# Causal mask of the pair attention: added by VectorE while it reads the scores, in place of four tensor products per step

## Chip, cores and metric

The kernel runs on 1 core of one Trainium2 chip. The metric is the device time of one execution in microseconds (us); several runs of a kernel are summed up by their median. The engines are TensorE (PE: matmuls, with its weight loads shown apart as PEld), VectorE (DVE), ScalarE (ACT), GpSimd (POOL) and SyncE (SP, which starts DMAs here). They run side by side and wait for each other on semaphores. Each engine works through its own instructions in program order.

## The reference

A tower of four transformer layers over 32 images of 37 tokens (36 patches and a class token), width 256, float32. Only two of its eight blocks after the embedding matter here: the attentions of layer 0 and of layer 2, both causal with 16 heads of 16 columns.

```python
# layer 0 (layer 2 is the same up to names and the layout of its weights)
att = jnp.einsum('bhqd,bhkd->bhqk', q, k) * (1.0 / jnp.sqrt(jnp.float32(D)))
causal = jnp.tril(jnp.ones((T, T), bool))
att = jnp.where(causal, att, -jnp.inf)
att = jax.nn.softmax(att, axis=-1)
y = jnp.einsum('bhqk,bhkd->bhqd', att, v)
...
h = _layernorm(h + _L0_attn_ref(h, ...), axis=-1)
```

## The kernel before

`tower` runs nine stages one after the other, separated by barriers: 0 the embedding, then attention and feed-forward block of each layer. `pair_attention` is stage 1 (layer 0, from about 36 to 142 us) and stage 5 (layer 2, from about 483 to 593 us).

**How the work is tiled.** An image has T = 37 rows; R = 111 rows are three images. `pair_attention` takes the 32 images in 16 pairs, one pair per step `s`; in the partition dimension one image of the pair stands in rows 0 to 36 and the other in rows 64 to 100 (PR = 101). Six images, three steps, are a unit `u = s // 3`. There are 18 steps (STEPS): a pair's work is spread over three steps, and the steps of different pairs overlap. All 16 heads of a pair have their scores at once, in four banks of PSUM (`scores`: 4 banks x 4 heads x 37 keys, 592 columns per row).

**What one pair needs, in order.** PE writes the scores (`score`: four matmuls that put the mask, 0 or -1e30, into the four banks, then 16 small matmuls that add the products of queries and keys). DVE takes each row's maximum (L469) and writes scores minus maximum to `P` in SBUF (L472); this is `shift`. ACT takes the exponential in place (`exps`, L412). PE transposes `P` in two halves (`p_T`, L613), ACT copies each half out (L417), PE multiplies with the values (`values`, L626), DVE divides by the sums (`normalise`, L480 and L483), PE transposes the result (`o_T`, L635), ACT copies it (L423).

**What a unit needs beside it.** PE: the transpose of the next unit's input (`x_T`, L555, step 3k), its query products (`q_project`, L563, step 3k), its key products (L563, step 3k+1) and its value products in two phases (`v_project`, L586, step 3k+2), and the output product of the unit before (`o_project`, L646, step 3k+1). DVE: `v_out` (L495, four additions, step 3k+2), which brings the values to SBUF, and `residual` (L504 to L510, step 3k+1 after the shift): residual and layer norm statistics. POOL: `norm` and `biased` (L358 to L363, L352), the layer norm of the unit before and its copy with a bias. Steps 3k, 3k+1 and 3k+2 are called x step, o step and v step below.

**What sets the order.** It is written out by hand, per engine. On PE a step is: `score(s)`, `p_T(s-1, 0)`, the unit's work, `o_T(s-2)`, `p_T(s-1, 1)`, more of the unit's work, `values(s-1)`. On DVE: `normalise(s-2)`, `shift(s)`, the unit's work. On ACT: copy of `p_T(s-1, 0)`, then others, copy of `o_T(s-2)`, copy of `p_T(s-1, 1)`, `exps(s)`. `score(s)` may overwrite the four banks once `shift(s-1)` has read them (semaphore `shifted`, which also releases the exponential).

Two things are in stage 1 alone: DVE prepares weights of the next stage (maxima L1679 in steps 3 and 4, 2.25 us each; conversions L541, with ACT's L455, in steps 12 to 16). In stage 5 alone PE transposes rows for a router (`routed_T`, L658) in step 16, which waits until all 16 shifts are done.

The mask comes by DMA with the stage's weights as `pair_mask` (101 x 37, float32). At the stage's start DVE converts it to bfloat16, four times side by side (L463), as the operand of the four matmuls.

## Time and profile before

| | |
|---|---|
| median of 3 runs | 1130.23 us (1118.12, 1130.23, 1132.64) |
| profiled execution, its own time | 1124.02 us |
| its span in the trace | 1122.2 us |
| mean granted TensorE clock | 0.898 |
| busy: PE / DVE / ACT / POOL | 963.6 / 590.2 / 487.1 / 321.8 us |
| mask matmuls L596 | 128, 14.7 us busy (a mean of 237 ns while they overlap) |
| score matmuls L603 | 16.0 us busy |
| shift: L469 and L472 | 24.6 us and 24.8 us busy, 32 of each |
| exponential L412 | 23.1 us busy, 32 |

The profile is one execution. A timeline row merges instructions of one kind that follow each other: start, the time from its first start to its last end, engine, line, what is written and read, and the count (a float32 matmul stands in it as two). Neighbouring rows of PE overlap by a little since matmuls are pipelined, so the distance from one start to the next is the time that a group costs. `[idle before <-releaser]` tells that the engine stood still and who ended it.

### The profile page before, as it was taken

Reading aid. Unit: us, or ns where it says so; the run is one execution under the profiler, and the core shown is the slowest. Engines: PE = TensorE matmul, PEld = TensorE weight load, DVE = VectorE, ACT = ScalarE, POOL = GpSimd, SP = SyncE. Lnnn points to the kernel's source line nnn. Section 1 sums busy time; section 2 is a strip of 40 time slices with the busy share of each in tenths; the row PEclk is TensorE's granted clock in tenths of the full one; section 3 lists DMA queues with packets and bytes.
Section 4 is the critical chain, followed back from the end, with each engine's and each line's share of the span. In section 5 each row is a group of like instructions: output and inputs, shape, how many; then the busy total and the mean of one; then the engine's idle time right before and its main releaser. Section 6 shows DMA issues by size and latency. Waiting matters only on the chain. (4 is left out here: it accounts for less than half of the span.)

```text
span 1122.2 us, 25634 instructions
## 1 busy us (share of the span) xinstructions
PE 963.6 (86%) x10184; PEld 719.9 (64%) x10184; DVE 590.2 (53%) x1279; ACT 487.1 (43%) x907; POOL 321.8 (29%) x423
## 2 busy tenths in 40 slices
PE   6899867899999799879996899999579999988664
PEld 6788625677777566658873466665267777777332
DVE  5576667566665298735656122211355456432585
ACT  3444477555555497634440122222113334422454
POOL 0213302444431000031320344442444545431101
PEclk9999888898999898889996899999788999986885
DMA  6200030200000100040007352332400000000001
GB/s 215 82 3 2 3 118 1 80 2 1 0 0 2 45 0 1 1 155 3 3 2 279 142 150 46 48 48 24 124 9 3 2 2 4 3 3 1 1 1 44
DMA packets 19657, 46.29 MB, mean 41 GB/s; under 512 B 4546, under 2 KB 10882, under 8 KB 18686
## 3 DMA queue, kind: packets, MB, share of 16 engines
q1 hardware_dynamic: 14300, 37.36, 9.4%
q0 software_dynamic: 4992, 6.82, 3.9%
q8 instruction: 79, 1.29, 0.5%
q10 hardware_dynamic: 256, 0.57, 0.2%
q14 instruction: 30, 0.25, 0.1%
HBM read 37.62 MB, written 7.12 MB: 40 GB/s over the span
## 5 line engine op out<-in xcount | busy, mean ns | idle before, releaser
L2620 DVE TENSOR_TENSOR weights_even<-psum,weights_even 128x512 f32<-128x512 f32 x26 | 18.0, 692 | 104.9 <-PE psum L2692 104.9
L2415 POOL DMA_INDIRECT expert_sums<-weights_even,L2f_target x26 | 41.1, 1583 | 93.2 <-DVE weights_even L2613 80.8
L1046 PE MATMUL psum<-L_cT,weights_odd 128*128 128x222 f32 (+1 forms) x192 | 49.5, 392 | 9.6 <-DVE L_by_sin L935 8.4
L2291 PE MATMUL psum<-weights_even,L1f_H 128*111 128x256 f32 x176 | 46.8, 424 | 7.5 <-DVE L1f_H L2222 7.5
L935 DVE TENSOR_TENSOR L_by_cos<-psum,vectors_odd 128x444 f32<-128x444 f32 (+1 forms) x48 | 26.6, 554 | 49.4 <-PE psum L1046 49.0
L2449 ACT ACTIVATE weights_even<-psum 128x256 f32<-128x256 f32 x26 | 10.0, 383 | 96.3 <-PE psum L2687 93.2
L2692 PE MATMUL psum<-gate_weights,weights_even 128*128 x104 | 50.8, 612 | 0.5 <-ACT weights_even L2449 0.5
L2725 PEld LDWEIGHTS psum<-L2f_EW,weights_even 128*128 128x128 f32 x208 | 39.4, 190 | 17.0 <-issue 13.0
L2725 PE MATMUL psum<-L2f_EW,weights_even 128*128 x208 | 49.2, 379 | 0.8 <-ACT weights_even L2454 0.8
L2692 PE MATMUL psum<-L2f_EW,weights_even 128*128 x104 | 49.9, 603 | 0.0
L874 ACT ACTIVATE L_PT<-psum 101x296 f32<-101x296 f32 x32 | 13.3, 416 | 80.7 <-PE psum L1087 80.0
L417 ACT ACTIVATE L_PT<-psum 101x296 f32<-101x296 f32 x64 | 26.9, 421 | 48.9 <-PE psum L613 48.9
L2291 PEld LDWEIGHTS psum<-weights_even,L1f_H 128*111 128x111 f32 x176 | 34.8, 200 | 18.4 <-DVE L1f_H L2222 8.7
L1046 PEld LDWEIGHTS psum<-L_cT,weights_odd 128*128 128x128 f32 x192 | 36.0, 215 | 15.8 <-issue 13.4
L358 POOL TENSOR_TENSOR L_rs<-L_mv,ln_eps 111x2 f32<-111x2 f32 (+1 forms) x12 | 3.0, 252 | 143.4 <-DVE L_mv L510 136.3
L155 PE MATMUL psum<-identb 128*128 128x512 bf16 x162 | 43.9, 434 | 0.0
L563 PE MATMUL psum<-L_xT,weights_odd 128*128 128x222 f32 (+1 forms) x192 | 41.0, 361 | 3.3 <-DVE L_V L495 1.9
L165 PE MATMUL psum<-decay_W_high,L1a_xT_high 128*111 128x512 f32 x88 | 39.3, 447 | 0.9 <-DVE L1a_xT_low L1344 0.9
L1119 PE MATMUL psum<-weights_odd,L_OT 128*111 128x256 f32 x176 | 39.2, 380 | 0.5 <-ACT L_OT L881 0.5
L613 PE MATMUL psum<-ident,L_P 101*101 101x101 f32 x256 | 37.1, 268 | 1.9 <-ACT L_PT L417 1.2
L800 POOL TENSOR_TENSOR L_P<-L_P,L_rc 101x592 f32<-101x592 f32 x16 | 19.2, 1198 | 68.2 <-DVE L_rc L953 68.2
L2273 PE MATMUL psum<-L1f_XT,weights_even 128*128 128x333 f32 (+1 forms) x128 | 36.9, 434 | 1.3 <-ACT L1f_XT L2114 0.7
(449 smaller groups left out, 2586.9 us busy)
## 6 DMA issues: line engine op xcount, KB each, us to landing
L2f_EW<-experts SPq DMA_DIRECT2D x16, 512.0 KB, 8.0
weights_even<-L_w SPq DMA_DIRECT2D x4, 1024.0 KB
gate_weights<-experts SPq DMA_DIRECT2D x8, 512.0 KB, 6.9
patch_ring<-patches SPq DMA_DIRECT2D x11, 333.0 KB, 7.0
weights_odd<-L_wqkv SPq DMA_DIRECT2D x2, 768.0 KB
out<-X SPq DMA_DIRECT2D x10, 111.0 KB
expert_rows<-X SPq DMA_DIRECT2D x1, 1056.0 KB, 4.9
expert_sums<-X SPq DMA_DIRECT2D x1, 1056.0 KB
```

Source lines behind the costliest of these rows:

```text
L155: core.nc.tensor.matmul(cols(core.bank(bank), 4, 128), core.identb[:], core.identb[:].unsqueeze(1).broadcast_to([128, 4, 128]), start=True ...
L165: mm = core.nc.tensor.matmul(out, left[a], right[b], start=first and n == 0, stop=last and n == len(passes) - 1)
L417: nc.scalar.activation(PT[:PR, s % 2, 4 * half:4 * half + 4].rearrange("p n (b q) -> p n b q", b=2), cols(core.bank(PTB)[:PR, 0:512], 4, 1 ...
L563: mm = nc.tensor.matmul(bank[:, c * NC2:c * NC2 + n], wqkv[:, kd, first + 128 * c:first + 128 * (c + 1)], xT[:, u % 2, kd, 0:n], start=kd ...
L613: mm = nc.tensor.transpose(core.bank(PTB)[:PR, 128 * i:128 * i + PR], P[:PR, s % 2, 2 * cq:2 * cq + 2].rearrange("p e k -> p (e k)")[:, 0: ...
L1046: mm = nc.tensor.matmul(bank[:, h * NC2:h * NC2 + width(u)], wu[:, (2 * g + h) * 128:(2 * g + h + 1) * 128], cT[:, u % 2, n // 4, 0:width( ...
L1119: mm = nc.tensor.matmul(core.bank(M2)[:R, m * D:(m + 1) * D], OT[:, c, first:first + R], wo[:, c, :], start=c == 0, stop=c == 7)
L2273: mm = nc.tensor.matmul(core.bank(bank)[:, 0:k * R], w1[:, kk, c * 128:(c + 1) * 128], XT[:, kk, group_cols(t0, k)], start=kk == 0, stop=k ...
L2291: mm = nc.tensor.matmul(y_bank(t), H[:, c, t * R:(t + 1) * R], w2[:, c, :], start=False, stop=c == nf - 1 and (t % 2 == 1 or t == NT - 1))
L2415: nc.gpsimd.indirect_dma_start(sums[:, :], bass.IndirectOffsetOnAxis(ap=target[:, j:j + 1], axis=0), Y[:, j % 2, :], None, compute_op=ALU. ...
L2692: mm = nc.tensor.matmul(core.bank(bank), xsT[:, j % 2, c, :], weights[:, expert[j], c * NF:(c + 1) * NF], start=c == 0, stop=c == KD - 1)
L2725: mm = nc.tensor.matmul(core.bank(5)[:, 0:D], HT[:, (j - 1) % 2, c * 128:(c + 1) * 128], EW[:, expert[j - 1], KD * NF + c * D:KD * NF + (c ...
```

## The change

Four edits in `pair_attention`, so in stages 1 and 5 alike:

- `score` loses its four mask matmuls; the 16 score matmuls start their own sums (`start=True, stop=True`).
- `shift` has three DVE instructions instead of two: scores plus mask, PSUM and SBUF to `P` (new L471); the row maximum of `P` (L473); `P` minus the maximum, in place (L475). A drain stands behind the first and the second.
- A semaphore `masked`, raised by the first of them, releases `score(s+1)`; it was `shifted`, raised by the last. The wait for `pt_ps` moves from ahead of the last instruction to ahead of the first.
- At the stage's start the conversion of the mask goes; DVE clears the four banks instead, once.

```diff
-        mask = sb("mask", [128, 4, T], BF16)
+        mask = w["pair_mask"]
...
-                nc.vector.tensor_copy(mask[:PR], w["pair_mask"].unsqueeze(1).broadcast_to([PR, 4, T])).then_inc(set_up, 1)
+                nc.vector.memset(scores, 0.0).then_inc(set_up, 1)
...
                     peaks = mx[:PR, s % 2].rearrange("p (j h) -> p j h", j=4)
-                    nc.vector.tensor_reduce(peaks, scores, AX.X, ALU.max)
+                    whole = P[:PR, s % 2].rearrange("p (j h) k -> p j h k", j=4)[:, :, :, 0:T]
+                    after(dve, pt_ps, 2 * (s - 1))
+                    nc.vector.tensor_tensor(whole, scores, mask.unsqueeze(1).unsqueeze(1).broadcast_to([PR, 4, 4, T]), ALU.add).then_inc(masked, 1)
                     dve.drain()
-                    after(dve, pt_ps, 2 * (s - 1))
-                    nc.vector.tensor_tensor(P[:PR, s % 2].rearrange("p (j h) k -> p j h k", j=4)[:, :, :, 0:T], scores,
-                                            peaks.unsqueeze(3).broadcast_to([PR, 4, 4, T]), ALU.subtract).then_inc(shifted, 1)
+                    nc.vector.tensor_reduce(peaks, whole, AX.X, ALU.max)
+                    dve.drain()
+                    nc.vector.tensor_tensor(whole, whole, peaks.unsqueeze(3).broadcast_to([PR, 4, 4, T]), ALU.subtract).then_inc(shifted, 1)
...
-                    after(pe, shifted, s)
-                    for j in range(4):
-                        nc.tensor.matmul(core.bank(S0 + j)[:PR, 0:4 * T], core.identb[:PR, :PR], mask[:PR].rearrange("p h k -> p (h k)"),
-                                         start=True, stop=False)
+                    after(pe, masked, s)
...
-                                                      start=False, stop=c == 1)
+                                                      start=True, stop=True)
```

PE of the kernel before, from the end of an o step through a v step to `o_T` of the next x step (here steps 4 to 6; L586 are the value products, L635 is `o_T`):

```order
L626 MATMUL psum<-L_V,L_PT 37x34 x16
L596 MATMUL psum<-L_mask,identb 101x148 x4
L603 MATMUL psum<-L_kT,L_qT 37x74 x16
L613 MATMUL psum<-ident,L_P 101x101 x4
L586 MATMUL psum<-weights_odd,L_xT 37x128 x12
L635 MATMUL psum<-ident,L_O 128x101 x2
L613 MATMUL psum<-ident,L_P 101x101 x4
L586 MATMUL psum<-weights_odd,L_xT 37x128 x12
L626 MATMUL psum<-L_V,L_PT 37x34 x16
L596 MATMUL psum<-L_mask,identb 101x148 x4
L603 MATMUL psum<-L_kT,L_qT 37x74 x16
```

The same stretch in the changed kernel:

```order
L625 MATMUL psum<-L_V,L_PT 37x34 x16
L602 MATMUL psum<-L_kT,L_qT 37x74 x16
L612 MATMUL psum<-ident,L_P 101x101 x4
L588 MATMUL psum<-weights_odd,L_xT 37x128 x12
L634 MATMUL psum<-ident,L_O 128x101 x2
L612 MATMUL psum<-ident,L_P 101x101 x4
L588 MATMUL psum<-weights_odd,L_xT 37x128 x12
L625 MATMUL psum<-L_V,L_PT 37x34 x16
L602 MATMUL psum<-L_kT,L_qT 37x74 x16
```

Each step has four matmuls less; nothing else of PE moved.

DVE of the kernel before, from `residual` of an o step through the v step to the next `normalise`, whose result `o_T` waits for (here steps 7 to 9, the first unit without the maxima of the weights; L495 is `v_out`):

```order
L504 TENSOR_TENSOR L_z<-psum,L_xb 111x512
L507 BN_STATS L_stat<-L_z 111x6 x2
L510 BN_AGGR L_mv<-L_stat 111x2 x2
L480 RECIPROCAL L_rd<-psum 101x16
L483 TENSOR_TENSOR L_O<-psum,L_rd 101x256
L469 TENSOR_REDUCE L_mx<-psum 101x16
L472 TENSOR_TENSOR L_P<-psum,L_mx 101x16x37
L495 TENSOR_TENSOR L_V<-psum,vectors_odd 37x24x16 x4
L480 RECIPROCAL L_rd<-psum 101x16
L483 TENSOR_TENSOR L_O<-psum,L_rd 101x256
```

And in the changed kernel:

```order
L506 TENSOR_TENSOR L_z<-psum,L_xb 111x512
L509 BN_STATS L_stat<-L_z 111x6 x2
L512 BN_AGGR L_mv<-L_stat 111x2 x2
L482 RECIPROCAL L_rd<-psum 101x16
L485 TENSOR_TENSOR L_O<-psum,L_rd 101x256
L471 TENSOR_TENSOR L_P<-psum,vectors_odd 101x16x37
L473 TENSOR_REDUCE L_mx<-L_P 101x16
L475 TENSOR_TENSOR L_P<-L_P,L_mx 101x16x37
L497 TENSOR_TENSOR L_V<-psum,vectors_odd 37x24x16 x4
L482 RECIPROCAL L_rd<-psum 101x16
L485 TENSOR_TENSOR L_O<-psum,L_rd 101x256
```

`shift` has one instruction more, of 592 columns like the other two, and its last one now reads two operands in SBUF (`P` and the maxima) where it read one in PSUM and one in SBUF.

## Rows read from the trace of the kernel before

**Rows 1.** The page's head: span and number of instructions.

```profile
span 1122.2 us, 25634 instructions
```

**Rows 2.** Stretches: from:to, length, busy us (instructions) by engine, PEclk, DMA, GB/s.

```profile
70.00:80.00 10.00, 8.68 (x207) 7.52 (x202) 9.45 (x18) 3.56 (x11) 4.77 (x6) 1.00 0.01 3
500.00:510.00 10.00, 8.55 (x131) 7.30 (x131) 4.49 (x8) 4.69 (x12) 0.00 (x0) 0.83 0.01 2
```

**Rows 3.** Timeline of PE, one unit of stage 5: start us, us, work [idle before].

```profile
522.12 0.46 PE L596 MATMUL psum<-L_mask,identb 101*101 101x148 bf16 x4
522.51 0.49 PE L603 MATMUL psum<-L_kT,L_qT 32*37 32x74 f32 x32
...
529.23 0.34 PE L635 MATMUL psum<-ident,L_O 101*128 101x101 f32 x2
529.61 0.57 PE L613 MATMUL psum<-ident,L_P 101*101 101x101 f32 x4
...
533.23 0.60 PE L613 MATMUL psum<-ident,L_P 101*101 101x101 f32 x4
...
538.59 0.46 PE L596 MATMUL psum<-L_mask,identb 101*101 101x148 bf16 x4
```

**Rows 4.** Timeline of DVE, the same unit.

```profile
521.53 0.69 DVE L504 TENSOR_TENSOR L_z<-psum,L_xb 111x512 f32<-111x512 f32 x1 [2.96 <-PE psum L646]
...
523.95 0.77 DVE L469 TENSOR_REDUCE L_mx<-psum 101x16 f32<-101x592 f32 x1
...
525.48 1.11 DVE L495 TENSOR_TENSOR L_V<-psum,vectors_odd 37x384 f32<-37x384 f32 x2
527.14 1.12 DVE L495 TENSOR_TENSOR L_V<-psum,vectors_odd 37x384 f32<-37x384 f32 x2 [0.55 <-PE psum L586]
...
528.63 0.43 DVE L483 TENSOR_TENSOR L_O<-psum,L_rd 101x256 f32<-101x256 f32 x1
```

**Rows 5.** Groups by line: out<-in, shapes, xcount | busy us, mean ns | idle before.

```profile
L472 DVE TENSOR_TENSOR L_P<-psum,L_mx 101x592 f32<-101x592 f32 x32 | 24.8, 776 | 2.8 <-issue 0.4
L469 DVE TENSOR_REDUCE L_mx<-psum 101x16 f32<-101x592 f32 x32 | 24.6, 770 | 7.4 <-PE psum L603 6.3
...
L951 DVE TENSOR_REDUCE L_rc<-L_P 101x16 f32<-101x592 f32 x16 | 12.3, 770 | 46.4 <-ACT L_P L869 46.4
...
L1386 DVE TENSOR_TENSOR L1a_la_low<-L1a_la,L1a_la_high 111x512 fp32r<-111x512 f32 x11 | 7.6, 693 | 5.5 <-ACT L1a_la_high L1317 5.5
...
L412 ACT ACTIVATE L_P<-L_P 101x592 f32<-101x592 f32 x32 | 23.1, 721 | 1.5 <-DVE L_P L472 1.5
```

**Rows 6.** Timeline of POOL, the same unit.

```profile
524.70 2.43 POOL L363 TENSOR_SCALAR X<-L_z,L_mv,L_rs 111x256 f32<-111x256 f32 x2 [0.18 <-issue]
```

**Rows 7.** DVE and POOL side by side: timelines near 198 and 37; L1256's min/median/max.

```profile
198.70 1.21 DVE L1348 TENSOR_TENSOR L1a_W_low<-weights_odd,decay_W_high 128x1024 fp32r<-128x1024 f32 x1
...
198.73 1.98 POOL L1256 TENSOR_SCALAR decay_xin<-decay_xin,L1a_prs 111x256 f32<-111x256 f32 x1 [0.18 <-issue]
...
L1256 POOL TENSOR_SCALAR decay_xin<-decay_xin,L1a_prs x10: 929/966/1982, 198.7 to 329.7; 111x256 f32<-111x256 f32 x10
...
36.72 3.48 DVE L463 CAST L_mask<-vectors_odd 101x148 bf16<-101x148 f32 x1
...
37.28 2.82 POOL L341 MEMSET L_V<- 128x3264 f32 x1
```

**Rows 8.** Timeline of PE at five other places of the two stages.

```profile
46.88 1.74 PE L563 MATMUL psum<-L_xT,weights_odd 128*128 128x222 f32 x8 [0.95 <-DVE L_V L495]
...
74.61 0.39 PE L635 MATMUL psum<-ident,L_O 101*128 101x101 f32 x2 [1.30 <-DVE L_O L483]
...
112.18 0.39 PE L635 MATMUL psum<-ident,L_O 101*128 101x101 f32 x2 [0.35 <-DVE L_O L483]
...
128.57 0.67 PE L613 MATMUL psum<-ident,L_P 101*101 101x101 f32 x4 [0.47 <-ACT L_P L412]
...
577.71 1.74 PE L658 MATMUL psum<-ident,X 111*128 111x111 f32 x16
```

More of the change, by code:

```diff
@@ L308, in pair_attention @@
         stat, mv, rs = sb("stat", [128, 2, 2, 6]), sb("mv", [128, 2, 2, 2]), sb("rs", [128, 2, 2])
-        mask = sb("mask", [128, 4, T], BF16)
+        mask = w["pair_mask"]
         bkm = sb("bkm", [128, 2, 2])
-        (xT_ps, xT_done, q_ps, q_done, k_ps, k_done, v_ps, v_done, s_ps, shifted, exp_done, pt_ps, pt_done, o_ps, o_done,
+        (xT_ps, xT_done, q_ps, q_done, k_ps, k_done, v_ps, v_done, s_ps, masked, shifted, exp_done, pt_ps, pt_done, o_ps, o_done,
          oT_ps, oT_done, y_ps, z_done, var_ready, norm_done, xb_done, zeroed, set_up) = st.sems(
-            "xT_ps xT_done q_ps q_done k_ps k_done v_ps v_done s_ps shifted exp_done pt_ps pt_done o_ps o_done "
+            "xT_ps xT_done q_ps q_done k_ps k_done v_ps v_done s_ps masked shifted exp_done pt_ps pt_done o_ps o_done "
             "oT_ps oT_done y_ps z_done var_ready norm_done xb_done zeroed set_up")
```

## The prediction

> **What bounds the kernel now.** Only two of nine stages change, so I read those two and let the rest of the span stand [rows 1]. The timeline of PE comes first. In the middle of stage 5 a unit of three steps lasts from 522.12 to 538.59, 16.47 us [rows 3], and no row of PE in it has an idle mark: PE bounds there. A mask group costs 522.51 - 522.12 = 0.39 us. Second, DVE of the same unit [rows 4]: it waits 2.96 us before `residual` (521.53), then works almost without a break until `normalise` ends at 528.63 + 0.43 = 529.06; the one pause is 0.55 us before the second half of `v_out`. `o_T` needs that result and starts at 529.23. So the slack of this path is 0.17 us, though DVE idles 3.5 us in these two pauses alone. That is the place which decides. Third, the spots where PE already waits for DVE or ACT [rows 8].
>
> **What is removed.** 32 mask groups (16 steps, two stages) of 0.39 us: 12.5 us if PE bounds everywhere. The conversion at the start of stage 1 took 3.48 us [rows 7], but it was over at 40.20, while PE was still at the first unit's projections (it reaches the second unit's at 46.88 [rows 8]); removing it gives nothing, and clearing the banks, one pass over 592 columns and below 1 us, hides there too.
>
> **What is added on DVE.** The add reads 592 columns from PSUM, as L472 does: 0.776 us. The maximum moves to SBUF: L951 has that very shape in SBUF and takes 770 ns, L469 from PSUM also 770. The last subtraction has two operands in SBUF: L1386 does this on 512 columns in 693 ns; 80 more columns at about 1.04 ns give 776 [rows 5]. Against 1.53 us for a shift (523.95 to 525.48 [rows 4]) that is one instruction of 0.776 and one drain more, which I take as 0.08: **+0.85 us per shift**. Bounds: 0.77 without the drain, 0.93 with two.
>
> The Trainium skill (VectorE: DVE Perf Modes, § The TRN2 errata) gives a Vector instruction a fixed part of 120 cycles when it reads PSUM and 58 when it reads SBUF. By it two of the three would be 0.065 us shorter, and the whole forecast some 1 us lower. The two rows of 770 ns speak against it, and the measurement decides.
>
> **The steady unit.** In the v step the chain `residual`, `normalise`, `shift`, four `v_out`, `normalise` grows by 0.85 and loses the pause of 0.55: +0.30, so the result comes at 529.36 and `o_T` at 529.46 instead of 529.23. PE, with two masks less in front, would be there at 528.45, and waits 1.0 us. Behind `o_T`, `p_T` started at 529.61 since it waited for ACT's copy; now the copy is early and it starts 0.23 after `o_T`, at 529.69: +0.08. So two of three masks are lost to this wait; only the third, at the end of the x step, is kept: -0.39 + 0.08 = **-0.31 us per unit**, where PE alone would give -1.18. The other DVE results have cover. In the x step the shift starts 0.34 after L483's successor, at 529.3, and ends at 529.3 + 2 x 0.85 + 0.78 = 531.78; the exponential takes 0.72 [rows 5], so `p_T` can start at 532.6; PE comes at 533.23 - 0.31 = 532.9. `masked` is raised long before the next score. The o step's shift lies in front of DVE's idle 2.96 us.
>
> **The port.** The new subtraction takes two operands from SBUF, and that has a price when POOL reads too. At 198.73 POOL's L1256 took 1.98 us instead of its usual 0.97, beside DVE's L1348 with two SBUF operands from 198.70 to 199.91: POOL stood until DVE was done [rows 7]. In the steady unit the subtraction comes at 523.95 + 2 x 0.85 = 525.65, inside POOL's first L363 (two of 1.22 from 524.70 [rows 6]), which ends at 525.92. If DVE gets in there, it has lost d = 0.27 us; if it loses to the second too, d = 1.5. Both are to be had by the rows: the conversion at 36.72 lasted until POOL's second memset was over, 40.10, so it lost to one that came later [rows 7]; at 198.70 the waiting engine went as soon as the other ended. I take 0.27, with 0 and 1.5 as the ends. This d adds straight to the chain before `o_T`. It is the rule of the Trainium skill (SBUF — State Buffer, § Who interferes with whom) that a Vector instruction with two SBUF inputs contends with a GpSimd one that reads SBUF, and that each fully blocks; the row at 198.73 agrees.
>
> **Stage 1, added up** (shift of PE against before). The second `v_out` stands behind the first shift, and PE waits for it at 46.88 already [rows 8]: +0.85 less the first mask, with a small gap, +0.54. The masks of steps 1 to 4 give back 1.56, of which a short wait before `o_T` keeps 0.13: -0.89 at the first `residual`. In steps 5 to 7 the maximum of a weight lies in DVE's chain, and PE already waits 1.30 us at 74.61 [rows 8]: the chain keeps its length plus 0.85, so the -0.89 is gone and one mask is left: -0.39. Next unit -0.31 + d: -0.70 + d. In the unit of step 11 PE waits at 112.18 already [rows 8], so nothing is hidden: +0.30 + d at `o_T`, and 0.15 more since the next exponential is late as well: -0.25 + 2d. In steps 14 and 15 two shifts follow each other in DVE's unbroken work, and `p_T` at 128.57 waits for the exponential [rows 8]: +1.70 + d. End of stage 1: **+1.45 + 3d**.
>
> **Stage 5.** The same start without the maxima: -0.94. Two units: -0.62 + 2d. Unit of step 11: the slack is nil, +0.06 + d. Then `routed_T`, at 577.71 [rows 8], waits for the sixteenth shift, two shifts of +0.85 later less 0.17 of slack: it moves from 577.71 to 578.4, +0.70 + d. End: **-0.80 + 4d**.
>
> Together +0.65 + 7d; with d = 0.27: **+2.5 us**. On the profiled execution (1124.02) that gives 1126.5. The four executions shown of before (1118.12, 1124.02, 1130.23, 1132.64) have a mean of 1126.3 and lie 14.5 us apart, more than any case below but one; I add to the mean: 1126.3 + 2.5 = **1129 us**. Measured against the median of 1130.23 it is no change.
>
> **Rivals.**
> - *DVE hides it, PE bounds throughout.* Then all 32 x 0.39 = 12.5 us come back: 1114. For it: DVE's idle 3.5 us per unit. Against it: nearly all of it lies before `residual`, not in front of `o_T`, where the slack is 0.17, and PE waits at 74.61 and 112.18 already. Chance 0.14.
> - *DVE loses the port each time* (slower). With d = 1.5: +0.65 + 10.5 = +11, 1137; if it loses also to L352 behind, d is about 2.9 and the sum +21, 1147. The seven are the v steps 8, 11 and 14 of stage 1 and 5, 8, 11 and 14 of stage 5. It takes d over 3.1 in all of them to pass 2%. For it: the conversion at 36.72; POOL's two L363 follow each other without a gap. Against it: 198.70. Chance 0.16.
> - *TensorE's clock falls in the new waits.* In the stretch from 500 it was granted 0.83 after waits of PE at the start of stage 5; from 70 to 80 it stayed at 1.00 in spite of the wait of 1.30 us [rows 2, 8]. A stretch of 10 us at 0.83 costs 1.7 us; in each of seven units 12 us: 1138. Chance 0.10.
> - *The sum above*, d from 0 to about 0.7 and shift from 0.77 to 0.93: the terms move by 4 us, the scatter of before by 7 to either side. Chance 0.60, own range 1119 to 1138.
>
> **How the numbers follow.** The range of 8 in 10 takes the forecast's scatter, part of the first rival from below and of the two slower ones from above: 1117 to 1143. What a measurement of this kernel can tell from no change is about 2%, 22.5 us. Faster by that needs nearly twice all masks: 0.03, for scatter. Slower needs the port lost throughout, or both slow rivals: 0.05. Within 2%: 0.92.
>
> **What the changed profile would show.** L471, L473 and L475 at 0.77 to 0.78 us each; L475 in v steps longer or late beside L363, and L363 longer. PE idle about 1 us before `o_T` in x steps, put down to DVE's L485; a unit of 16.1 to 16.5 us. If a unit is 15.3 us, the first rival holds; at 17.6 the second. `routed_T` with a wait for L475 in front. Stage 1 ends 1.5 to 3 us later, stage 5 within 1 us. I am wrong at the root if L475 is cheaper than 0.7 us or if DVE's order lets `o_T` through earlier.

## The result and the profile after

The changed kernel was compared with the one before three times, each time with a set of executions of the kernel before taken for that comparison.

| comparison | changed kernel, median us (lowest to highest) | before, median us | ratio, 95% interval |
|---|---|---|---|
| first (4 executions each) | 1141.51 (1135.02 to 1148.13) | 1128.84 | 1.0126 [1.0077, 1.0175] |
| second (12 and 35) | 1135.23 (1130.57 to 1154.78) | 1128.95 | 1.0035 [0.9994, 1.0076] |
| third (12 and 35) | 1133.64 (1130.04 to 1151.81) | 1129.40 | 1.0039 [1.0000, 1.0079] |

So the change costs 4 us (0.35 and 0.39%) by the two larger comparisons, whose intervals just reach 1, and 14 us (1.3%) by the first, which has four executions on each side. The forecast was 1129 us: 2.5 us of added time on a base of 1126.3, called no change against the median of 1130.23. Of every kernel here, the one before too, a part of the executions is 1.5 to 3% longer at a lower granted clock; the comparisons leave these out, which four executions hardly allow, and by their clock the profiled ones of the first comparison (1148.13 us, 0.874) and of the third (0.871), of the changed kernel with fill in all waits (0.883) and of the kernel before with late statistics (0.878) are of that kind, while that of the second (0.887) is not.

The head of the page after ([rows 1] has 25634 instructions and a span of 1122.2 us):

```profile
span 1146.3 us, 25470 instructions
```

VectorE's three instructions of a shift, from the groups by line (shapes, count, busy us, mean ns, idle before):

```profile
L475 DVE TENSOR_TENSOR L_P<-L_P,L_mx 101x592 f32<-101x592 f32 x32 | 25.5, 796 | 2.4
L473 DVE TENSOR_REDUCE L_mx<-L_P 101x16 f32<-101x592 f32 x32 | 24.6, 770 | 2.9
L471 DVE TENSOR_TENSOR L_P<-psum,vectors_odd 101x592 f32<-101x592 f32 x32 | 24.6, 768 | 6.5 <-PE psum L602 6.4
```

All three cost what the prediction had taken. The 796 ns of L475 is a mean with one outlier; 770 to 780 ns is what nearly all of them show. TensorE in the steady unit of stage 5 that answers to [rows 3] (start us, length us, then the work, in brackets the idle time before it and what ended it):

```profile
541.76 0.77 PE L625 MATMUL psum<-L_V,L_PT 101*37 101x34 f32 x32
...
548.40 0.55 PE L557 MATMUL psum<-ident,X 111*128 111x111 f32 x4
549.79 0.39 PE L634 MATMUL psum<-ident,L_O 101*128 101x101 f32 x2 [0.85 <-DVE L_O L485]
...
557.78 0.77 PE L625 MATMUL psum<-L_V,L_PT 101*37 101x34 f32 x32
```

`values` to `values` is 557.78 - 541.76 = 16.02 us, before 16.47. The mask groups are gone, and in front of `o_T` there is the wait of 0.85 us put down to `normalise` (L485), where [rows 3] shows none. VectorE and GpSimd (POOL) in the v step of that unit, answering to [rows 4] and [rows 6]:

```profile
544.28 0.77 DVE L471 TENSOR_TENSOR L_P<-psum,vectors_odd 101x592 f32<-101x592 f32 x1
...
545.98 0.78 DVE L475 TENSOR_TENSOR L_P<-L_P,L_mx 101x592 f32<-101x592 f32 x1
546.68 2.27 DVE L497 TENSOR_TENSOR L_V<-psum,vectors_odd 37x384 f32<-37x384 f32 x4
...
549.31 0.42 DVE L485 TENSOR_TENSOR L_O<-psum,L_rd 101x256 f32<-101x256 f32 x1
```

```profile
545.04 2.81 POOL L363 TENSOR_SCALAR X<-L_z,L_mv,L_rs 111x256 f32<-111x256 f32 x2 [0.18 <-issue]
```

L475 takes 0.78 us beside POOL's L363, and L363's pair takes 2.81 us where [rows 6] has 2.43: POOL stood, not VectorE. Taken one by one, the pair's first instruction, begun at 545.04 before L475, took its usual 1.22 us, and the second, begun at 546.26 while L475 was running, took 1.59.

**Where the time went.** The two changed stages can be measured from their first VectorE instruction (L461) to their last `residual` (L504 before, L506 after). Before:

```profile
36.57 0.23 DVE L461 TENSOR_TENSOR L_bkm<-vectors_odd 128x2 f32<-128x2 f32 x2 [0.69 <-PEq L131]
...
139.79 0.42 DVE L504 TENSOR_TENSOR L_z<-psum,L_xb 111x256 f32<-111x256 f32 x1
...
483.82 0.23 DVE L461 TENSOR_TENSOR L_bkm<-vectors_odd 128x2 f32<-128x2 f32 x2 [0.77 <-PEq L131]
...
589.72 0.42 DVE L504 TENSOR_TENSOR L_z<-psum,L_xb 111x256 f32<-111x256 f32 x1 [4.48 <-PE psum L646]
```

That is 103.22 us in stage 1 and 105.90 us in stage 5. The same in the second comparison's profile of the changed kernel:

```profile
36.53 0.23 DVE L461 TENSOR_TENSOR L_bkm<-vectors_odd 128x2 f32<-128x2 f32 x2 [0.69 <-PEq L131]
...
144.34 0.42 DVE L506 TENSOR_TENSOR L_z<-psum,L_xb 111x256 f32<-111x256 f32 x1 [0.99 <-PE psum L645]
...
492.18 0.23 DVE L461 TENSOR_TENSOR L_bkm<-vectors_odd 128x2 f32<-128x2 f32 x2 [0.77 <-PEq L131]
...
601.25 0.42 DVE L506 TENSOR_TENSOR L_z<-psum,L_xb 111x256 f32<-111x256 f32 x1 [4.34 <-PE psum L645]
```

107.81 and 109.07 us: 4.6 and 3.2 us more. By the same reading:

| profile | stage 1, us | stage 5, us | of it: units from `residual` to `residual` in stage 5 |
|---|---|---|---|
| before | 103.22 | 105.90 | 16.47, 16.47, 15.06, **13.21**, 6.98 |
| changed, first | 113.40 | 109.02 | 16.02, 16.02, 15.17, **17.83**, 6.99 |
| changed, second | 107.81 | 109.07 | 16.02, 16.02, 15.17, **17.84**, 7.01 |
| changed, third | 113.39 | 109.08 | 16.02, 16.02, 15.18, **17.83**, 7.03 |

Three profiles agree within 0.1 us in stage 5: the steady units are 0.45 us shorter each, and the unit from step 13 to step 16 is 4.6 us longer. That unit is where stage 5 loses. The stages 2 to 4, which are the same code, took from 344 us (before, 139.79 to 483.82) over 348 (second profile) to 355 us (first profile, 149.78 to 504.88); no reading below uses them.

Not all of stage 1's 4.6 us is the change's. The first 16 projections of TensorE (L563 before, L565 after) stand ahead of every scores product. In the kernel before, in the second profile of the changed one, and in another kernel that is unchanged up to there (experiment 5), they read:

```profile
37.83 3.27 PE L563 MATMUL psum<-L_xT,weights_odd 128*128 128x222 f32 x16 [0.70 <-ACT L_xT L386]
```

```profile
37.80 4.96 PE L565 MATMUL psum<-L_xT,weights_odd 128*128 128x222 f32 x16 [0.70 <-ACT L_xT L386]
```

```profile
37.73 4.87 PE L566 MATMUL psum<-L_xT,weights_odd 128*128 128x222 f32 x16 [0.69 <-ACT L_xT L386]
```

The same work takes 1.6 to 1.7 us longer at half clock for a part of it: from 36 to 46 us the granted clock is 1.00 in the first, 0.83 in the two others. It came with unchanged code too, so the change need not be its cause, and why it comes in one execution and not in another is open. The same holds for the stage's last unit: 5.35 us before, 6.28 changed, but also 6.29 in the kernel before with late statistics and with one longer wait (experiments 6 and 5), where its last output product takes 2.05 us for 1.32, as in the changed kernel.

TensorE of the first profile in stage 5's unit of 17.83 us:

```profile
593.37 0.49 PE L602 MATMUL psum<-L_kT,L_qT 32*37 32x74 f32 x32
594.77 0.60 PE L612 MATMUL psum<-ident,L_P 101*101 101x101 f32 x4 [0.91 <-ACT L_P L412]
...
596.62 1.07 PE L625 MATMUL psum<-L_V,L_PT 101*37 101x34 f32 x32
597.98 3.22 PE L657 MATMUL psum<-ident,X 111*128 111x111 f32 x16 [0.29 <-DVE L_P L475]
600.99 0.89 PE L612 MATMUL psum<-ident,L_P 101*101 101x101 f32 x4
```

and the stretches around it (from:to, length, busy us with instructions of PE, PEld, DVE, ACT, POOL, then the granted clock), of after and of before:

```profile
585.00:595.00 10.00, 8.71 (x182) 7.16 (x183) 7.66 (x16) 5.12 (x16) 3.67 (x4) 1.00 0.01 2
595.00:605.00 10.00, 9.15 (x73) 7.75 (x73) 3.27 (x7) 4.11 (x12) 0.75 (x2) 0.61 0.01 2
```

```profile
574.00:584.00 10.00, 9.05 (x166) 7.61 (x160) 4.41 (x10) 4.78 (x14) 1.81 (x2) 1.00 0.01 2
```

After the wait of 0.91 us in front of `p_T` (step 15; ACT's exponential is late since VectorE's shift of step 14 is) the clock goes from 1.00 to 0.61 in the mean of ten microseconds, that is to its lower level (1.2 of 2.4 GHz) for most of them. `routed_T` (L657) takes 3.22 us where [rows 8] has 1.74 for the same sixteen transposes, and `p_T` behind it 0.89 where it takes 0.52 at full clock. Before, the stretch that holds `routed_T` was granted 1.00 throughout.

### The profile page after: what moved, and what is told of

It is laid out like the page before. It is cut to its first block and busy times, and to the rows that moved or that the text cites. A ratio compares the mean times of both kernels' runs of the same rounds, so it can differ in the third digit from the quotient of the medians.

```text
span 1146.3 us, 25470 instructions
## 1 busy us (share of the span) xinstructions
PE 977.5 (85%) x10056; PEld 731.8 (64%) x10056; DVE 610.8 (53%) x1311; ACT 489.3 (43%) x907; POOL 324.3 (28%) x423
## 5 line engine op out<-in xcount | busy, mean ns | idle before, releaser
L565 PE MATMUL psum<-L_xT,weights_odd 128*128 128x222 f32 (+1 forms) x192 | 46.7, 399 | 5.3 <-DVE L_V L497 3.9
L565 PEld LDWEIGHTS psum<-L_xT,weights_odd 128*128 128x128 f32 x192 | 39.8, 231 | 7.3 <-issue 4.2
L155 PE MATMUL psum<-identb 128*128 128x512 bf16 x162 | 43.1, 428 | 0.0
L165 PE MATMUL psum<-decay_W_high,L1a_xT_high 128*111 128x512 f32 x88 | 41.9, 476 | 0.9 <-DVE L1a_xT_low L1343 0.9
```

Source lines behind the costliest of these rows:

```text
L155: core.nc.tensor.matmul(cols(core.bank(bank), 4, 128), core.identb[:], core.identb[:].unsqueeze(1).broadcast_to([128, 4, 128]), start=True ...
L165: mm = core.nc.tensor.matmul(out, left[a], right[b], start=first and n == 0, stop=last and n == len(passes) - 1)
L565: mm = nc.tensor.matmul(bank[:, c * NC2:c * NC2 + n], wqkv[:, kd, first + 128 * c:first + 128 * (c + 1)], xT[:, u % 2, kd, 0:n], start=kd ...
```

## The experiments

Three theories. **One**: TensorE's longer waits behind VectorE's longer chain let its clock fall, and that is most of the loss. **Two**: the chain itself costs it, and the falls of the clock are scatter. **Three**: it is the work that TensorE no longer has that brings the clock down. The table that the sections refer to, each from one profile, ratio from the timed executions:

| kernel | stage 1 | stage 5 | steady unit | step 13 to 16 unit of stage 5 | ratio, 95% interval |
|---|---|---|---|---|---|
| before | 103.22 | 105.90 | 16.47 | 13.21 | 1 |
| changed (second) | 107.81 | 109.07 | 16.02 | 17.84 | 1.0035 [0.9994, 1.0076] |
| vector half alone | 108.92 | 106.61 | 16.46 | 13.93 | 1.0037 [0.9996, 1.0079] |
| tensor half alone | 99.72 | 98.65 | 15.29 | 12.55 | 0.9900 [0.9827, 0.9972] |
| changed, fill in all waits | 104.05 | 105.82 | 16.05 | 14.59 | 0.9950 [0.9904, 0.9995] |
| changed, one fill | 107.73 | 104.73 | 16.02 | 13.94 | 1.0019 [0.9983, 1.0055] |
| changed, late statistics | 102.17 | 107.51 | 15.29 | 17.73 | 0.9999 [0.9963, 1.0035] |
| the same, one fill | 102.83 | 103.63 | 15.29 | 13.93 | 0.9979 [0.9945, 1.0014] |
| the same, fill at start and end | 101.37 | 102.07 | 15.29 | 14.71 | 0.9907 [0.9866, 0.9947] |
| before, late statistics | 104.24 | 105.86 | 16.47 | 13.21 | 0.9992 [0.9948, 1.0037] |
| before, fill at start and end | 106.31 | 107.29 | 16.47 | 14.66 | 1.0009 [0.9970, 1.0049] |
| before, one longer wait | 107.17 | 109.49 | 16.46 | 16.89 | 1.0025 [0.9995, 1.0056] |

Stage 1's times differ between kernels by 1.5 to 1.7 us, and once by 3.0, because of its first projections alone. They take 3.27 or 3.28 us in the profiles of before, both halves, fill in all waits, late statistics and late statistics with one fill; 4.80 to 4.96 us in the three of the changed kernel and those with one fill, before with late statistics, before with one longer wait, late statistics with fill at start and end; and 6.29 us in before with fill at start and end. In the profile of before the first `residual` comes 33.29 us after the stage's start, in before with one longer wait 34.89 us, and nothing else of TensorE differs up to there.

**1. The vector half alone.** The changed kernel, with TensorE's four products put back on top:

```
+        maskb = sb("maskb", [128, 4, T], BF16)
...
                     after(pe, masked, s)
+                    for j in range(4):
+                        nc.tensor.matmul(core.bank(S0 + j)[:PR, 0:4 * T], core.identb[:PR, :PR],
+                                         maskb[:PR].rearrange("p h k -> p (h k)"), start=True, stop=False)
```

> The vector half of the change alone: VectorE runs the three instructions (add mask, maximum, subtraction) and releases the scores' banks after the first, but TensorE still multiplies the mask in with its four products (so the mask is added twice, which leaves the result as it was). Theory 1 (TensorE's longer waits behind VectorE's longer chain let its clock fall, and that is most of the loss): as slow as the changed kernel or slower, 1.010 to 1.020 of the kernel before, half clock after longer waits in steps 5 to 12 of stage 1 and at the start of both attention stages. Theory 2 (the chain itself costs everything, 0.85 us per step where it binds, the falls of the clock are scatter): 1.008 to 1.015, with stage 1 longer by the chain at full clock. Theory 3 (less work on TensorE alone brings the clock down): TensorE has all its work here, so no more falls of the clock than before and 1.000 to 1.004.

Measured: 1.0037, below what theories one and two asked for and inside the range of three; it is also as slow as the whole change (1.0035 and 1.0039). The steady unit says why. It is 16.46 us, as before: the mask groups on TensorE cover the 0.85 us that VectorE needs longer, and the waits of `o_T` add up to 7.9 us where the changed kernel has 12.0 and 12.7 in its first two profiles, and the kernel before 4.6. So this kernel does not have "the same waits with more work", as its expectation assumed. In the unit of step 13 to 16 of stage 5:

```profile
584.43 0.60 PE L616 MATMUL psum<-ident,L_P 101*101 101x101 f32 x4
...
587.63 1.74 PE L661 MATMUL psum<-ident,X 111*128 111x111 f32 x16 [0.45 <-DVE L_P L476]
```

The `p_T` of step 15 (584.43) has no wait of note, and `routed_T` takes 1.74 us, full clock. This run does not decide between one and three.

**2. The tensor half alone.** The kernel before without the four products; VectorE has its two instructions. The causal mask is left out here.

```
-                    for j in range(4):
-                        nc.tensor.matmul(core.bank(S0 + j)[:PR, 0:4 * T], core.identb[:PR, :PR],
-                                         mask[:PR].rearrange("p h k -> p (h k)"), start=True, stop=False)
...
-                                                      start=False, stop=c == 1)
+                                                      start=True, stop=True)
```

> The tensor half of the change alone: the four products with the mask are gone and VectorE keeps its two instructions; the causal mask is left out of the computation. Theory 1: TensorE's waits for VectorE grow by at most 0.31 us per step and seldom pass 1 us, so no more falls of the clock than before, and a time of 0.985 to 0.998 of the kernel before. Theory 2: the same, 0.990 to 0.998. Theory 3 (less work on TensorE brings its clock down): stage 1 longer by 5 to 10 us at a clock below 0.9 in its later half, 1.004 to 1.010.

Measured: 0.9900, and the two stages 3.5 and 7.3 us shorter. The steady unit is 15.29 us: 16.47 less three mask groups (1.18). Theory three is out in this form: with the same work taken from TensorE the clock of that unit stays up, and `routed_T` takes its 1.74 us:

```profile
572.30 0.39 PE L632 MATMUL psum<-ident,L_O 101*128 101x101 f32 x2 [0.20 <-DVE L_O L483]
...
574.18 1.74 PE L655 MATMUL psum<-ident,X 111*128 111x111 f32 x16
```

Together the halves say how the parts combine. Over both stages the tensor half gives -10.8 us and the vector half +6.4; their sum would be -4.4, the whole change is +7.8. Of the 12 us between, 3.9 are the half clock behind step 14 (experiment 4) and 1.7 that of the first projections, which neither half's profile has. The rest is what each half covers for the other: TensorE's gain is only there if VectorE's chain does not grow, and the chain's growth is only hidden if TensorE keeps the masks.

**3. Fill in TensorE's waits.** The changed kernel with products that nobody reads (128 x 512, four take 1.04 us) where it waits: six before the second `q_project`, four before `o_T` in steps 6, 9, 12, nine in steps 15 and 16.

```
+                    if s in (15, 16):
+                        pe.wait_ge(z_done, 4)
+                        keep_busy(core, M2, 4 if s == 15 else 3)
                     if 1 <= s <= NP:
                         p_T(s - 1, 0)
...
+                    if s == 15:
+                        keep_busy(core, M2, 2)
+                    if s % 3 == 0 and 3 < s < 15:
+                        pe.wait_ge(v_done, v_phases(u + 1))
+                        keep_busy(core, M2, 4)
                     if s >= 2:
                         o_T(s - 2)
...
+                    if s == 0:
+                        pe.wait_ge(xT_done, 2)
+                        keep_busy(core, M1, 6)
                     if u + 1 < NU and s % 3 == 0:
                         q_project(u + 1)
```

> The changed kernel with products that nobody reads put into TensorE's waits: six before the second projection of Q, four before the transpose of O in the steps 6, 9 and 12, a few in the last steps of both attention stages. VectorE's chain stays as long as in the changed kernel. Theory 1: the clock stays at 0.95 or more from 50 to 130 us, stage 1 takes 108 to 111 us in place of 118, and the time is 0.997 to 1.005 of the kernel before. Theory 2: no gain, 1.011 to 1.018, since the chain is as long and the fill delays the transposes by up to 0.2 us. Theory 3 gives the same as theory 1, but without a fall before the longest waits.

Measured: 0.9950 [0.9904, 0.9995], faster than the kernel before and outside all the ranges named, on the fast side. VectorE's chain is as long as in the changed kernel, and the steady unit stays at 16.05:

```profile
562.87 1.04 PE L155 MATMUL psum<-identb 128*128 128x512 bf16 x4
563.74 0.34 PE L634 MATMUL psum<-ident,L_O 101*128 101x101 f32 x2
```

so what came back is not the chain's length. The unit of step 13 to 16 of stage 5 is 3.2 us shorter in spite of nine products on top, the same unit of stage 1 is 1.75 us shorter (14.82 for 16.57 in the second profile), and stage 1 takes 104.05 us in place of 107.81 to 113.40; 1.5 to 1.7 us of that lie in the first projections, ahead of any fill. This goes against theory two as the whole explanation. It does not explain the time, though: the two stages add up to 209.87 us here and to 209.12 before, so the 5.6 us (0.5%) by which this kernel was timed faster than before are not found in them.

**4. One fill.** Only the four products in front of `p_T` in step 15.

```
+                    if s == 15:
+                        pe.wait_ge(z_done, 4)
+                        keep_busy(core, M2, 4)
                     if 1 <= s <= NP:
                         p_T(s - 1, 0)
```

> The changed kernel with four products that nobody reads in one place of each attention stage: TensorE's wait of 0.91 us before the transpose of P in step 15. Theory 1: that one wait starts the half clock in the last unit of stage 5; with the fill the clock stays at 1.00 there and the last unit takes 13.2 to 14.2 us in place of 17.83, 3 to 4 us less in all than the changed kernel. If other, shorter waits are enough, the last unit stays at 17 us or more.

```profile
581.31 1.04 PE L155 MATMUL psum<-identb 128*128 128x512 bf16 x4
582.28 0.60 PE L612 MATMUL psum<-ident,L_P 101*101 101x101 f32 x4
...
584.14 0.90 PE L625 MATMUL psum<-L_V,L_PT 101*37 101x34 f32 x32
585.49 1.74 PE L657 MATMUL psum<-ident,X 111*128 111x111 f32 x16 [0.45 <-DVE L_P L475]
```

The rows are those of the changed kernel's unit with L155 where the wait of 0.91 us was, and every length is back at full clock: `values` 0.90 for 1.07, `routed_T` 1.74 for 3.22. The unit takes 13.94 us for 17.83, stage 5 takes 104.73 us for 109.07. From 584 to 594 the granted clock is 1.00. The time, 1.0019, is 0.2% below the changed kernel's 1.0035 and 1.0039; the intervals overlap, so for this one the profile carries the verdict. Experiment 7 has the same fill once more, on top of late statistics, with the same effect (17.73 to 13.93). In stage 1 the same fill changed nothing (107.73).

**5. One longer wait in the kernel before.** VectorE's maximum of step 14 is taken three times; nothing else.

```
+                    for _ in range(2 if s == 14 else 0):
+                        nc.vector.tensor_reduce(peaks, scores, AX.X, ALU.max)
+                        dve.drain()
```

> The kernel before with VectorE's maximum of step 14 taken three times in place of once (the result is the same), so that TensorE waits about 1.2 us longer before one transpose of P in each attention stage, while it does all its work, the mask too. Theory 1 (a wait of this length at this place is enough for the half clock): the last unit of stage 5 takes 16.5 to 18.5 us in place of 13.2 and the time is 1.002 to 1.007 of the kernel before. If it takes the missing work as well (theory 3), the clock stays at 1.00, the last unit takes 14.0 to 14.8 us, and the time is at most 1.003.

```profile
577.72 0.77 PE L629 MATMUL psum<-L_V,L_PT 101*37 101x34 f32 x32 [0.29 <-ACT L_OT L423]
579.62 0.43 PE L599 MATMUL psum<-L_mask,identb 101*101 101x148 bf16 x4 [1.14 <-DVE L_P L475]
579.99 0.53 PE L606 MATMUL psum<-L_kT,L_qT 32*37 32x74 f32 x32
580.45 1.00 PE L616 MATMUL psum<-ident,L_P 101*101 101x101 f32 x4
...
584.18 3.16 PE L661 MATMUL psum<-ident,X 111*128 111x111 f32 x16
587.18 0.52 PE L616 MATMUL psum<-ident,L_P 101*101 101x101 f32 x4
```

The wait came out before the mask group of step 15 (1.14 us, [1.14 <-DVE L_P L475]) and not before `p_T`. Behind it `p_T` takes 1.00 us for 0.60 and `routed_T` 3.16 for 1.74; from 587.18 on the lengths are normal again. The unit takes 16.89 us (13.21 before), the kernel 1.0025, which lies in the ranges of both theories, so the unit decides. TensorE does all of its work here, masks too: a wait of that length at that place is enough, and theory three falls. Together with experiment 4 this shows theory one for stage 5: put the wait in and the half clock comes, fill the wait and it goes.

**6. Late statistics.** The other way to take the waits away: an earlier `normalise`. Of `residual` only the addition stays in the o step; the two BatchNorm statistics and aggregations move into the x step two steps later, behind its shift (those of the last units of a stage stay where they were). In stage 1 the maximum of a weight in step 4 also moves ahead of the addition, so the first `residual` stands behind it there.

```
+                def statistics(u):
+                    p, n = u % 2, len(UNITS[u][1])
                     dve.drain()
...
                     if s % 3 == 1 and u >= 1:
                         residual(u - 1)
+                        if s >= 13:
+                            statistics(u - 1)
+                    if s % 3 == 0 and 6 <= s <= 12:
+                        statistics(u - 2)
```

> The changed kernel with VectorE's statistics of the residual (two bn_stats, two bn_aggr) moved from the o step, where they stand ahead of the next steps' work, into the x step that has less to do; the addition itself stays. The wait of the transpose of O in x steps is taken away by an earlier start of VectorE's chain, not by fill. Theory 1: waits of 0.85 to 1.7 us in the middle of the stages go, so do the falls of the clock behind them; unit of stage 5 at 15.2 to 15.9 us (16.02 in the changed kernel), time 0.988 to 1.002 of the kernel before. Theory 2 (the chain alone): the unit gets shorter all the same, 4 to 8 us less than the changed kernel, 1.004 to 1.009. If the addition of 0.85 us has its price in the other steps too, the unit stays at 16.0 and the time at 1.010 or more.

```profile
541.87 0.39 PE L642 MATMUL psum<-ident,L_O 101*128 101x101 f32 x2
...
549.87 0.77 PE L633 MATMUL psum<-L_V,L_PT 101*37 101x34 f32 x32
...
570.10 0.60 PE L620 MATMUL psum<-ident,L_P 101*101 101x101 f32 x4 [0.91 <-ACT L_P L412]
...
573.30 3.22 PE L665 MATMUL psum<-ident,X 111*128 111x111 f32 x16
```

`o_T` starts without a wait, and the steady unit is 15.29 us, the same as with the tensor half alone: there all of TensorE's gain is kept and all of VectorE's added work is hidden. Stage 1 is at 102.17 us. But the unit of step 13 to 16 in stage 5 is still 17.73 us (the wait before `p_T` is again 0.91, and `routed_T` behind it takes 3.22), and the time is 0.9999 [0.9963, 1.0035]: no better than before, and 0.4% below the changed kernel's with intervals that overlap.

Control, the same move in the kernel before:

> Control for the moved statistics: the kernel before with the same move of VectorE's statistics out of the o step. In the kernel before TensorE bounds the unit at 16.47 us, so the unit stays at 16.4 to 16.5 and the time at 0.997 to 1.003 of the kernel before; if the move has an effect of its own (on POOL's norm, on ScalarE), the time leaves that range and the gain of the late statistics in the changed kernel is not due to the wait of the transpose of O.

Unit 16.47 us and 0.9992: in the kernel before the move does nothing, since no wait of `o_T` stands there to be removed.

**7. Both.** Late statistics with the one fill of experiment 4:

> The changed kernel with late statistics and with the four products in step 15 alone. Theory 1: unit 15.3 us, last unit of stage 5 at 13.2 to 14.5 us in place of 17.73, 0.990 to 0.997 of the kernel before. If the gain of the version with all fills (0.991) came from the fills at the start and in the last steps of stage 1, this one stays at 0.997 to 1.003.

The unit of step 13 to 16 goes from 17.73 to 13.93 us, stage 5 to 103.63; but the time, 0.9979, lies in the range that was named for the case that the gain of fill comes from other places too, and its interval holds 1. Late statistics with fill in all the places that are left (six products before the second `q_project`; two, five and three before `p_T` in steps 14 to 16; two before `o_T` in steps 15 and 16; in stage 1 six before the last `o_T`):

> The changed kernel with late statistics and with products that nobody reads in the waits that are left: before the second projection of Q, and in the last four steps. Theory 1: unit 15.3 us as with late statistics alone, last units without half clock (15 us in place of 16.3 in stage 1 and 17.7 in stage 5), time 0.984 to 0.994 of the kernel before. If the falls of the clock at the ends are not due to waits, the fill only lengthens the ends, 0.997 to 1.003.

0.9907 [0.9866, 0.9947], median 1120.89 for 1128.95: the fastest kernel of the study that computes the mask, ahead of both. Its two stages are 5.7 us shorter than before's and 3.0 us shorter than with the one fill; the medians differ by 8 us from before's, and what lies outside the two stages was not looked into. Control, fill in the kernel before at the start and in steps 15 and 16:

> Control for the fill: the kernel before with the products that nobody reads before the second projection of Q and in the last steps, none in the middle. Theory 1 for the change (its own longer waits are what the fill healed): the fill gives the kernel before less than it gave the changed one, 0.993 to 1.001. If the fill gives here as much as it did there (0.990 or less), the gain of the fill says nothing of the change's waits.

1.0009: the fill gives nothing here, where the fill of experiment 3 took the changed kernel from 1.004 to 0.995. Stage 5 is 1.4 us longer; of stage 1's 3.1 us 3.0 lie in its first projections (6.29 us for 3.27), ahead of any fill. This speaks for fill healing something that the change brought, but the control is not exact: experiment 3 has fill in the x steps too.

**8. The changed kernel again**, twice:

> The changed kernel once more, unaltered, because its loss so far rests on four executions whose mean granted clock (0.874 to 0.889) lies at the lower end of what the kernel before shows (0.868 to 0.903), while the vector half alone gave 1.004 with TensorE's four products still in it. Theory 1 (the waits lower the clock every time): 1.008 to 1.017 again. Theory of scatter (the four executions were drawn low): at most 1.004. If it comes out at 1.01 again while the vector half alone, with the same waits and more work, stays at 1.004, then the work that TensorE no longer has is part of the cause (theory 3).

> The changed kernel a third time, unaltered: its two comparisons with the kernel before gave 1.0126 and 1.0035, and their intervals hardly meet. If the loss is the one that both profiles of the changed kernel show in the last unit of stage 5 (17.8 us for 13.2) and in stage 1 (4.6 us in one, 10.2 in the other), it is 1.003 to 1.013 here too, never below 1.000.

Both came out at 1.004. By the first expectation that is scatter's range (at most 1.004) and not theory one's (1.008 to 1.017): the first comparison's 1.3% did not come again. The third comparison is inside what the second expectation names (1.003 to 1.013). The last sentence of the first expectation leads nowhere, since the vector half alone does not have the same waits (experiment 1).

So theory one holds for stage 5, where it is shown. The second profile's 7.8 us over before come apart like this: 3.9 are the half clock behind step 14 of stage 5 (17.84 less 13.94); 1.7 and 0.9 are half clock in the first projections and the last unit of stage 1, which profiles of unchanged code have too; the 1.2 us that are left (+1.97 in stage 1, -0.73 in stage 5) are theory two's, the longer chain of VectorE less the masks that TensorE saves. 3.9 and 1.2 are 5.1 us, of which the clock is the larger part, and the two larger comparisons have 4.

## Why the prediction was wrong, step by step

It said no change, 1129 us, with 2.5 us more work on the path; the change costs 4 to 14 us, a loss. The first comparison's 1141.51 lies inside the stated range, 1117 to 1143; what failed is the direction, and the term behind it. Held against the profiles:

- *Costs of the instructions.* Right: 768, 770 and mostly 0.78 us for the three, and 546.68 - 544.28 = 2.40 us from a shift's start to the next work, 0.87 more than the old 1.53 where 0.85 was taken. By its table of fixed parts the Trainium skill (VectorE: DVE Perf Modes, § The TRN2 errata), which says itself that the one for SBUF comes out too short, would have had the two instructions that read SBUF shorter than the one that reads PSUM; L473 reads SBUF and takes 770 ns, as L469 did from PSUM [rows 5], so the measurement does not bear it out here.
- *The steady unit.* Right in kind and nearly in size: the wait before `o_T` is 0.85 us and put down to L485, the unit 16.02 us; forecast was a wait of 1.0 and 16.16 + d.
- *The port.* d was taken as 0.27 us in seven places, 1.9 us of the sum. It was 0 in the steady v steps: POOL waited, its pair was 0.38 us longer. That POOL and a Vector instruction with two SBUF inputs get in each other's way is what the Trainium skill has (SBUF — State Buffer, § Who interferes with whom). The trace agrees (1.59 us for 1.22 of the L363 at 546.26); the prediction had only the wrong one waiting. Once in each profile VectorE was the one to stand: at 76.73 in stage 1 of the first, beside an L352 that began 0.01 us before it, L475 took 1.36 us; that v step is not among the seven. In both places the one that began second stood, but an L363 that had begun 0.95 us before L475 did not hold it up. The term was too large, and the slower rival built on it did not come.
- *Stage 5 up to step 13.* The three units give -0.45, -0.45 and +0.11 us, forecast -0.31 + d twice and +0.06 + d. With d = 0 this fits.
- *`routed_T`, the step that failed.* The sum has "+0.70 + d" for it, a pure delay by two longer shifts. It measured +4.6 us. (The 0.70 does not follow from its own sentence: two shifts of 0.85 less 0.17 are 1.53, and a start at 578.4 for 577.71 would make the stage end 0.70 later, not 0.80 earlier. As the unit's own growth at full clock it comes out at +0.73, with one fill.) The delay is there (waits of 0.91 before `p_T` and 0.29 before `routed_T`), but the first of these waits also starts a stretch at half clock, in which the same work takes almost twice as long (3.22 us for 1.74). The prediction had the mechanism as a rival with chance 0.10, priced at 1.7 us in each of seven units; it neither looked at where a wait would meet TensorE's end of the stage nor put a price on that place. In every profile of the changed kernel it came in the one unit behind step 14 of stage 5, for 3.9 us (17.83 less the 13.94 with one fill), and in none in the middle units of that stage.
- *Stage 1.* Forecast +1.45 + 3d, measured +4.6 (second profile) and +10.2 (first and third). In the second, behind the first `residual`: units of 18.78, 16.02, 15.97, 16.57 and 6.28 us for 17.84, 16.46, 15.20, 15.08 and 5.35, that is +0.94, -0.44, +0.77, +1.49, +0.93, where the working had +0.50, -0.31 + d, +0.45 + d and +1.70 + d for the last two. The first four, 2.8 us, are VectorE's chain where PE had no slack; the 1.5 of the fourth come out the same with the same fill in both kernels (14.82 and 13.32 us, experiments 3 and 7), at full clock. The 0.9 of the last unit is half clock, for unchanged code has 6.29 us there too. Ahead of the first `residual` the prediction had -0.89; +0.90 was measured, and of that 1.7 is the half clock of the first projections, so that -0.8 is left. With these two set aside stage 1 has +2.0 us, against a forecast of +1.45 with d = 0. In the first and third profile 5.6 us come on top, in units of 20.41 and 19.66 us for 18.78 and 15.97, at half clock in part (from 115 to 125 us the granted clock is 0.55 in the first, 1.00 in the second); whether the change's waits bring it is not shown.
- *Which rival held.* By the tensor half alone, "PE bounds throughout" would have been right for 10.8 of 12.5 us had VectorE's work been placed otherwise; experiment 6 places it so and has the unit of 15.29 us. In the kernel as changed the argument against that rival, no slack in front of `o_T`, was right.
- *The sum against the runs.* The chain alone was forecast at +0.65 with d = 0, and 1.2 us were found; so the working of the chain was good, the 1.9 us of the port were too much, and 3.9 us of clock, which stood at nothing in the sum, were missing. The 3.9 us are shown by experiments 4 and 5. In all, 2.5 us were forecast; the second and third comparison have 6.3 and 4.2 between medians, the first 12.7. How much of the first is the clock in stage 1, and how much the draw of four executions, is left open.

## What to carry to other kernels

Work taken from the engine that bounds is worth only what the engine that takes it over can hide in front of the next wait; count idle time there, not per unit, and move what nobody waits for (here the statistics) behind what somebody does. A new wait of TensorE must be priced twice, once as a delay and once with the work behind it at half clock; here the place was a stage's end, where waits of 0.29, 0.91 and 0.21 us follow each other closely. Before a difference between two profiles is put down to a change, look for rows of unchanged work that differ in it (here 4.96 for 3.27 us in the first projections). Both repairs can be tried cheaply: fill the one wait, or put it alone into the kernel before.

## What the runs showed that was not expected

Two waits of the same kind at the same place, before `o_T` in step 12 of stage 1, in two executions of the same code. First profile, then second:

```profile
115.29 0.39 PE L634 MATMUL psum<-ident,L_O 101*128 101x101 f32 x2 [1.55 <-DVE L_O L485]
...
115.88 1.84 PE L565 MATMUL psum<-L_xT,weights_odd 128*128 128x74 f32 x8
117.64 1.23 PE L625 MATMUL psum<-L_V,L_PT 101*37 101x34 f32 x32
```

```profile
114.16 0.39 PE L634 MATMUL psum<-ident,L_O 101*128 101x101 f32 x2 [1.76 <-DVE L_O L485]
...
114.75 1.03 PE L565 MATMUL psum<-L_xT,weights_odd 128*128 128x74 f32 x8
115.71 0.77 PE L625 MATMUL psum<-L_V,L_PT 101*37 101x34 f32 x32
```

The shorter wait (1.55 us) is followed by half clock, 1.84 us for a projection that takes 1.03; the longer one (1.76 us) is not. In stage 5 a wait of 0.90 or 0.91 us was followed by half clock in all three profiles of the changed kernel, and one of 1.04 us, before `o_T` one unit earlier, in none (569.15 in the second profile; the projection behind it takes its 1.03 us). So the length of a single wait does not tell whether the clock falls; what does, these runs leave open. And one instruction, VectorE's subtraction with both operands in SBUF, took its plain 0.78 us beside a POOL instruction that had begun before it (545.98 against 545.04 above); the POOL instruction that began during it was 0.38 us longer instead.
